# Routing of a two-choice expert layer: the first tile's gathers issued inside the routing block, and the second choice's lane masks made on GpSimd

## The reference

```
def _L0_ffn_ref(x, gate_w, expert_w):
    TOP_K = 2
    E = expert_w.shape[0]
    gate_logits = jnp.einsum('bsh,he->bse', x, gate_w)
    top_vals, top_idx = jax.lax.top_k(gate_logits, TOP_K)
    probs = jax.nn.softmax(top_vals, axis=-1)
    onehot = jax.nn.one_hot(top_idx, E, dtype=x.dtype)
    w_e = jnp.einsum('bsk,bske->bse', probs, onehot)
    expert_out = jnp.einsum('bsh,eho->bseo', x, expert_w)
    out = jnp.einsum('bseo,bse->bso', expert_out, w_e)
    return out
...
x = x + _L0_attn_ref(_layernorm(x, axis=-1), ...)
x = x + _L0_xattn_ref(_layernorm(x, axis=-1), ctx_4096, ...)
x = x + _L0_ffn_ref(_layernorm(x, axis=-1), L0_ffn_gate_w, L0_ffn_expert_w)
```

## Time and profile before

| | us |
|---|---|
| median of 3 runs | 1114.65 |
| lowest and highest of them | 1114.28 to 1115.48 |
| the profiled execution, its own time | 1115.55 |
| its span, first to last instruction | 1113.7 |
| mean granted clock of PE over the span | 0.951 |
| PE busy in the span | 1004.9 (90%) |
| DVE, POOL, ACT busy | 555.0, 447.8, 375.1 |
| end of the routing block (barrier) | about 581.9 |
| first product of the expert block | 592.19 |
| last product's end | 1100.60 |

### The profile page before, as it was taken

One profiled execution on the slowest core, in us unless ns is written; L12 is line 12 of the kernel. 1 busy time (PEld: TensorE's weight loads), 2 busy tenths in 40 slices (PEclk: granted clock), 3 DMA queues, 4 the chain that ended last, 5 costly groups with the idle time before them and its releaser, 6 DMA issues. The chain is left out here.

```text
span 1113.7 us, 13360 instructions
## 1 busy us (share of the span) xinstructions
PE 1004.9 (90%) x3534; PEld 531.0 (48%) x3535; DVE 555.0 (50%) x1660; ACT 375.1 (34%) x1016; POOL 447.8 (40%) x567
## 2 busy tenths in 40 slices
PE   5788889998998969799829999999999999999995
PEld 5687455564545435335514444444444444444442
DVE  5645779899997788978973111111111111111111
ACT  2334677786775328748820000000000000000000
POOL 3842455464653010008606433444333333333331
PEclk9878889999999989899958999999999999999998
DMA  7320111010000331003786473464637355373332
GB/s 300 119 92 3 49 49 38 30 67 1 1 1 1 152 114 39 1 1 155 296 322 232 89 227 79 128 182 129 176 76 229 77 138 163 75 226 75 75 76 38
DMA packets 38462, 120.25 MB, mean 108 GB/s; under 512 B 6220, under 2 KB 9351, under 8 KB 38408
## 3 DMA queue, kind: packets, MB, share of 16 engines
q1 hardware_dynamic: 25592, 79.77, 19.4%
q0 software_dynamic: 12816, 39.86, 16.4%
HBM read 82.91 MB, written 36.70 MB: 107 GB/s over the span
## 5 line engine op out<-in xcount | busy, mean ns | idle before, releaser
L2059 PE MATMUL bank<-T,X 128*128 x1184 | 508.4, 592 | 0.1
L2059 PEld LDWEIGHTS bank<-T,X 128*128 128x128 f32 x1184 | 224.9, 190 | 283.4 <-issue 283.4
L2121 DVE TENSOR_SCALAR X<-bank,col_p 128x512 f32<-128x512 f32 x37 | 27.8, 751 | 393.2 <-PE bank L2059 393.2
L2087 ACT ACTIVATE X<-bank,col_p 128x512 f32<-128x512 f32 x37 | 25.4, 688 | 495.1 <-PE bank L2059 467.0
L2010 POOL DMA_INDIRECT X<-x_nrm,col_s x156 | 150.4, 964 | 74.1 <-issue 47.2
L2019 POOL DMA_INDIRECT out_dram<-X,col_d x37 | 60.0, 1622 | 262.9 <-DVE X L2121 254.8
L479 POOL TENSOR_TENSOR rs<-ve,neg_half 128x4 f32<-128x4 f32 x36 | 37.5, 1041 | 114.7 <-DVE ve L960 114.7
L826 ACT ACTIVATE M<-X,T 128x256 bf16<-128x256 f32 x152 | 74.9, 495 | 2.0 <-POOLq L475 2.0
L645 PE MATMUL bank<-nat,T 128*128 128x512 f32 x128 | 64.0, 623 | 10.0 <-issue 7.4
L656 PE MATMUL bank<-X,T 128*128 128x512 f32 x128 | 62.5, 613 | 0.0
L2107 DVE STREAM_TRANSPOSE X<-X 128x1024 f32<-128x1024 f32 x39 | 48.4, 1240 | 27.4 <-DMA X<-x_nrm,col_s 16.9
(11 more groups left out here) (340 smaller groups left out, 1440.7 us busy)
## 6 DMA issues: line engine op xcount, KB each, us to landing
T<-in_L_ffn_expert_w_dram SPq DMA_DIRECT2D x8, 4096.0 KB, 17.6
out_dram<-X SPq DMA_DIRECT2D x17, 512.0 KB
M<-in_x_dram SPq DMA_DIRECT2D x16, 512.0 KB, 7.2
X<-in_x_dram SPq DMA_DIRECT2D x16, 512.0 KB, 6.6
x_nrm<-H SPq DMA_DIRECT2D x16, 512.0 KB, 3.0
T<-in_ctx_dram SPq DMA_DIRECT2D x9, 512.0 KB, 3.5
X<-x_nrm,col_s POOLq DMA_INDIRECT x156
X<-in_ctx_dram SPq DMA_DIRECT2D x4, 512.0 KB, 7.0
```

The source lines that it names most:

```text
L2059: mm = nc.tensor.matmul(bank[2 * u + n][:, :], xgt[u][:, k, :], Tf[:, ds(odd * D + (k * N + n * BANK), BANK)], start=(k == 0), stop=(k == ...
```

## The change

- DVE makes the 16 lane masks of the first choice only. Those of the second choice are made by POOL with the same operation, once `lane` is written (a semaphore wait on the 22nd step of the routing chain). PE's second group of token matmuls waits for POOL's last one.
- DVE's order behind the masks: four steps of the probabilities, then the copy `tok_parts`, two more steps, `src_i`, and then, still in the routing block, the rest of the pieces, all six `weighted`, the small tables and the transpose of slot 0. These stood in the expert block, or ahead of `tok_parts` and `src_i`.
- POOL issues the four gathers of slot 0 in the routing block, from `src_i` itself, behind the same waits as before.
- PE makes the matmuls of the probabilities in the routing block, with four matmuls on constants ahead of each group; the seven ahead of the products are gone.
- SP issues the last seven tiles of `out` at the start of the expert block, no longer at the end of the routing block.

```diff
@@ @block.sync (routing block)
                 sp.dma_start(out[N:N + P, :], X[:, 0, :]).then_inc(out_init, 16)
-                for t in range(KEPT_TILES, NT):
-                    sp.wait_ge(x2_done, 4 * (t // CT) + 2 + t % CT + 1)
-                    sp.dma_start(out[t * P:(t + 1) * P, :], X[:, t, :]).then_inc(out_late, 16)
@@ @block.gpsimd (routing block, at its end)
+                hold(pool, r_dve, LANES_SET)
+                pool.wait_ge(r_sel, QK + 1)
+                for t in range(NT):
+                    ins = nc.gpsimd.tensor_scalar(hot_lane[1][:, t, :], lane_row, lane[:, 1, t:t + 1], None, ALU.is_equal)
+                ins.then_inc(g_pool, 1)
+                for u in range(2):
+                    pool.wait_ge(nrm_st[u], B * 16)
+                pool.wait_ge(out_init, KEPT_TILES * 16 + 32)
+                hold(pool, src_set, 1)
+                for c in range(QK):
+                    nc.gpsimd.indirect_dma_start(out=xg[0][:, c * QD:(c + 1) * QD], out_offset=None, in_=x_quarters,
+                                                 in_offset=bass.IndirectOffsetOnAxis(ap=src_i[:, 0, c:c + 1], axis=0)).then_inc(xg_in[0], 16)
@@ @block.tensor (routing block)
                     pe.wait_ge(hot_set, k + 1)
+                    if k == 1:
+                        pe.wait_ge(g_pool, G_KNOWN + B - FIRST_SQUARED + 1)
...
+                for k in range(2):
+                    keep_busy(0, 4)
+                    pe.wait_ge(p_set, k + 1)
+                    for t in range(NT):
+                        mm = nc.tensor.matmul(bank[PROB][:, 0:3 * WIDE], hot_lane[k][:, t, :], of_prob[k][:, t, :, :].rearrange("p a s -> p (a s)"),
+                                              start=(k == 0 and t == 0), stop=(k == 1 and t == NT - 1))
+                mm.then_inc(p_mm, 1)
@@ @block.vector (routing block)
-                v.tensor_copy(lane[:, :, :], lane_i[:, :, :])
+                route(v.tensor_copy(lane[:, :, :], lane_i[:, :, :]))
+                assert n_route[0] == LANES_SET
...
+                    ins = v.tensor_tensor(of_token[k][:, :, 1, 0:SLOTS], at_slot[k][:, :, 0:SLOTS], tile_base[:, :, 0:SLOTS], ALU.mult)
+                    if k == 1:
+                        ins.then_inc(hot_set, 1)
+                        break
                     for t in range(NT):
                         ins = v.tensor_scalar(hot_lane[k][:, t, :], lane_row, lane[:, k, t:t + 1], None, ALU.is_equal)
...
                 weigh(dve, v.tensor_copy(piece[0], prob[:, :, :]))
+                dve.wait_ge(r_pe, 3)
+                v.tensor_copy(tok_parts[...], bank[TOKEN][...]).then_inc(tok_set, 1)
                 weigh(dve, v.tensor_tensor(prob_rest[0], prob[:, :, :], piece[0], ALU.subtract))
                 weigh(dve, v.tensor_copy(piece[1], prob_rest[0]))
-                weigh(dve, v.tensor_tensor(prob_rest[1], prob_rest[0], piece[1], ALU.subtract))
-                weigh(dve, v.tensor_copy(piece[2], prob_rest[1]))
-                dve.wait_ge(r_pe, 3)
...
-                for j in range(2):
-                    weighted(0, j)
                 dve.wait_ge(r_pe, 4)
                 route(v.tensor_scalar(src_i[...], bank[SOURCE][...], quarter[:, 0:1], None, ALU.add))
+                dve.sem_inc(src_set, 1)
+                weigh(dve, v.tensor_tensor(prob_rest[1], prob_rest[0], piece[1], ALU.subtract))
+                weigh(dve, v.tensor_copy(piece[2], prob_rest[1]))
+                for j in range(3):
+                    ins = weighted(0, j)
+                ins.then_inc(p_set, 1)
...
+                for j in range(3):
+                    ins = weighted(1, j)
+                ins.then_inc(p_set, 1)
+                turned(dve, 0, 0, 0)
@@ @block.sync (expert block)
                 sp.sem_inc(w_ready, 1)
+                for t in range(KEPT_TILES, NT):
+                    sp.wait_ge(x2_done, 4 * (t // CT) + 2 + t % CT + 1)
+                    sp.dma_start(out[t * P:(t + 1) * P, :], X[:, t, :]).then_inc(out_late, 16)
                 sp.wait_ge(xg_tp, 2)
@@ @block.gpsimd (expert block)
-                for u in range(2):
-                    pool.wait_ge(nrm_st[u], B * 16)
-                pool.wait_ge(out_init, KEPT_TILES * 16 + 32)
-                for u in range(IN_FLIGHT):
+                for u in range(1, IN_FLIGHT):
                     gather(u, u)
@@ @block.tensor (expert block)
                 pe.sem_inc(tile_mm, 1)
-                for k in range(2):
-                    pe.wait_ge(p_set, k + 1)
...
-                for i in range(7):
-                    nc.tensor.matmul(bank[0][...], ident[...], dense, start=(i == 0), stop=(i == 6))
                 with pe.Fori(0, ITER) as i:
```

More of the change, by code:

```diff
@@ L2100, in _ @@
                 v = nc.vector
-                def turned(j, i, u):
-                    hold(dve, xg_in[u], i * (QK * 16) + QK * 16)
-                    if not isinstance(j, int) or j >= IN_FLIGHT:
-                        hold(dve, tile_mm, j - IN_FLIGHT + 2)
-                    v.transpose(xgt_blocks[u], xg_blocks[u]).then_inc(xg_tp, 1)
                 def sources(j, u):
```

71 lines of the change are left out of this document (32 added, 39 removed).

## The result

| | before | after |
|---|---|---|
| median, us (10 runs each) | 1115.34 | 1118.31 |
| lowest to highest | 1112.19 to 1116.70 | 1116.75 to 1119.24 |
| the profiled execution, its own time | 1115.55 | 1119.09 |
| its span | 1113.7 | 1117.3 |
| mean granted clock of PE | 0.951 | 0.951 |

The ratio is 1.003, with a 95% interval of 1.002 to 1.0039: the kernel became 3 us slower. The forecast was 1114.2 with a range to 1117.2, and it gave "slower" 0.11. The time lies outside the range.

A forecast was written before the change was run, and what follows sets the result against it. Bound: PE's unbroken products from 592.19, their start held by SP's writes ahead of the barrier and gather and transpose latency behind it. Starting at 589.6 gains 2.6, the cold clock takes 2.1: 1114.65 - 0.5 = 1114.2 us, range 1111.9 to 1117.2.

The forecast's parts named there:

- DVE idle until 573.9, because `e2` comes from ACT.: Without its masks DVE is free at 571.4 but waits for ACT's `e2` until 573.9, so 2.5 us bring nothing.
- POOL's masks at 0.27 each, bounds 0.25 to 0.46, last one at 573.0.: POOL's 16 masks in the routing take 4.3 us at 0.27 each and stay covered, being needed by 573.5.
- A pause while DVE works.: POOL may stand still while DVE is busy until 571.4, ending its masks at 575.8; the middle, 573.0, was taken.
- Rival 4: POOL's masks starve beside DVE, last one 575.8 to 578.9, so slower than before: 1116.5 to 1119.6; chance 0.12.
- `tok_parts` to `src_i`'s end, 1.43; that to the first gather, 1.12; gather to transpose, 7.45.: Routing chain: `tok_parts` at 574.9, `src_i` ended at 576.33, first gather 577.45, transpose of slot 0 from 584.9.
- POOL's drain, 4.3 from the last issue.: At the barrier POOL drains 4.3 from the last gather's issue at 583.0, until 587.3, past DVE's 586.2.
- Barrier and PE's set-up, 0.54 and 1.9.: Behind the transpose, barrier latency 0.54, then PE's loop set-up, register loads and issue, 1.9, move from hidden to exposed.
- Cold clock, 2.1, bounds 1.5 to 2.8.: First products run at 1.2 GHz for 4.2 us until the clock rises, losing 2.1.
- Rival 2: The clock is up when the products start: 1112.0 with the drain (chance 0.13), 1111.0 without it (0.05).
- SP's writes are covered in the expert block.: SP's seven writes run 587.6 to 595.6; slot 1's gathers, expert 1's load and the first scatter are still in time.
- The sum.: First product from 592.19 to 589.6 gains 2.6, the clock takes 2.1: 0.5 us less, 1114.2.
- The forecast's order of waits: Time follows the products' start: list, gathers, transpose, barrier with POOL's drain, PE's set-up, first product at 589.6.

The follow-up runs named there:

- e1: The changed kernel with the second choice's 16 lane masks back on DVE, nothing else: 1115.50, ratio to before 1.000.
- e7: e1 plus sixteen matmuls on constants, eight at the end of PE's routing and eight ahead of the product loop: 1114.50, ratio to before 0.999.
- e4: The kernel before with SP's seven writes of `out` moved behind the barrier, to the start of the expert block: 1116.67, ratio 1.001.
- e5: The kernel before with only the second choice's lane masks moved to POOL: 1115.71, ratio 0.9998.
- e13: e6 with the second choice's 16 masks on POOL and PE's wait for them: 1114.98, ratio to before 0.9998.
- e6: The kernel before with SP's seven writes in the expert block, behind a wait for slot 0's transpose: 1111.98, ratio 0.9967.
- e11: e6 plus four and six matmuls on constants in PE's two idle stretches: 1113.48, ratio to before 0.9979.
- e10: e6 plus the early list, half the second choice's masks on POOL, e11's added constants and five ahead of the loop: 1110.06, ratio to before 0.9957.
- e3: e1 with slot 0's transpose moved into the expert block, behind the lists of slots 1 and 2: 1113.88, ratio to before 0.9983.

## Why the prediction was wrong, step by step

- *DVE idle until 573.9, because `e2` comes from ACT.* Right: the idle time is there, 2.08, ended by ACT.
- *POOL's masks at 0.27 each, bounds 0.25 to 0.46, last one at 573.0.* **This is the step that failed.** They take 0.60 with DVE idle, 2.4 times the row that I put them nearest to and above both of my bounds. The rows were a one-input operation that reads nothing (an IOTA) and a two-input one in fp32. I took "no tensor input" for "one input", and neither has a second operand fetched by a pointer or a bf16 output. Which of these makes the 0.6 was not measured. The last mask came at +11.80, 3.8 past the point from which, by the forecast, each microsecond counts.
- *A pause while DVE works.* The step that weighed it was of the right kind and measured 2.2 of the 11.4 us. The Trainium skill ("SBUF — State Buffer", Who interferes with whom) has the two engines block each other fully when DVE is in a two-port mode, or has two SBUF inputs while GpSimd's instruction reads SBUF. The two masks beside DVE's TENSOR_TENSOR (1.20 and 1.44 against 0.60) agree with what it says of two inputs. The masks of the two engines ran beside each other at 0.70 for POOL's and 2.83 for DVE's sixteen, against 0.60 and 2.68, so DVE's TENSOR_SCALARs and POOL's did not shut each other out for their whole length, as I had read the rule, and the measurement decides. Whether DVE's ran in a two-port mode is not in the trace. Rival 4 gave the right direction and place (the last mask later than 573.5), but not by its mechanism: the masks did not starve, they are dear. That its price fits (1116.5 to 1119.6, measured 1118.31) is luck.
- *`tok_parts` to `src_i`'s end, 1.43; that to the first gather, 1.12; gather to transpose, 7.45.* 1.43, 1.12 and 7.68. Right; only their start was 3.9 late. In e1, where it was nearly on time, the transpose stood at +20.04 against a forecast of +19.4.
- *POOL's drain, 4.3 from the last issue.* Wrong. It ends 0.2 behind the landing of the gathers and ahead of DVE's transpose, so here it costs nothing, and the 1.0 that my sum had for it was not there. The 4.3 at the kernel's end is there again (4.311), with everything landed, and is not what a drain behind four gathers costs.
- *Barrier and PE's set-up, 0.54 and 1.9.* From the transpose's end to the first product it took 2.97 in after, 3.0 in e1. I had 2.44 without the drain (and by my own rows the 1.9 in it was 1.7 + 0.1 = 1.8). PE's register loads are slower there: the longest of the second kind took 0.79, and 0.32 at most in before.
- *Cold clock, 2.1, bounds 1.5 to 2.8.* 1.57, shown by e7. The size is near its lower bound: the products ran at the lower clock for 3.2 us, not 4.2. The way there was another: I had the clock low throughout, but it rose at 587.18, under the constants, and fell at 590.59, at the barrier. Rival 2 had the rise right and the fall not.
- *SP's writes are covered in the expert block.* Right for the changed kernel. I had written nothing of what they do to gathers beside them, and e4 shows how near that was: had slot 0's gathers stood in that block, 3 us.
- *The sum.* First product: the late list +3.9 (3.3 of it against masks on DVE, by e1), gather to transpose +0.2, barrier, set-up and drain -0.5, so +3.6 on the forecast's +24.1. Clock -0.5. That is 3.1 above the forecast's -0.5, the 2.6 found in the trace. The remaining 1.0 between 1114.2 and 1118.31 is mostly the base: before's median was 1114.65 in the three runs I started from, and 1115.34 in the ten beside after.

The forecast's order of waits survives. In e1, with the masks back on DVE, the first product stands at +24.29, forecast +24.1. That the two lie so close is partly luck: the transpose was 0.6 late and PE's set-up 0.5 longer, and the 1.0 of the drain that did not come made up for both. What was wrong is that two rows of other operations were taken as ends for a price that had no row. The threshold was there: with the last mask needed at 573.5, 0.48 for one decides, just past my upper end of 0.46, and the value above it was given to one rival at 0.12.

## What to carry to other kernels

- Before an operation goes to POOL, look for a row of the same operation, operand kinds and type there. Where there is none, compute from which price on it decides (here 0.48 for a mask: 7.6 us for 16) and say how likely that is, rather than settle between two rows of other operations.
- A step that costs nothing today may be hidden by the very thing that the change removes. The masks cost nothing with SP's writes ahead of the barrier (e5) and 3 us without them (after, e13). Measure the parts of a change alone and together.
- Moving plain writes off one path puts them beside something else. Ask which latency-bound transfer runs in that time, and let them wait for its end: one semaphore made 4.7 us here (e4, e6).
- Matmuls that raise the clock should also fill the time up to the first real one: with an idle stretch of 2.02 us behind them the clock fell again and the products took 1.1 us longer (e11); with stretches of at most 1.19 (e7) and 0.27 (e10) it stayed up. Elsewhere it stayed up through 2.07 in one execution and fell in another, so look at more than one profile.

## What the runs showed of the hardware beyond that

- A POOL TENSOR_SCALAR of 128 x 128 bf16 with a column as its scalar took 0.593 to 0.597 us in each of the nine masks that it made while DVE made none (after, e13), and 0.70 beside DVE's masks. One of DVE's takes 0.17.
- POOL's drain behind the gathers took 6.60, 6.44, 6.57 and 6.43 us in after, e1, e3 and e7, counted from its start in the queue, most of it beside the gathers themselves, and ended 0.2 behind the last landing.
- Seven writes of 512 KB on the hardware queue (DMA share 1.01, 384 GB/s) lengthened gather to transpose from 7.4 to 10.4 us.
- Products beside DMA engines that are full lost nothing: 508.40 in e7 (share 1.00 to 1.02) and e13 (0.97 over the first 8 us), as in before (0.51).
- Upstream of the change the granted clock differs from execution to execution (0.95 or 1.00 over the same 130 us), which moves positions by up to 4 us. Positions relative to a common instruction remove that.
